# Attention block on one core: the third batch's statistics on ACT, eight split value units, and stores and row spreads moved off SP's queue

## The reference

```python
h = _group_norm(x, gn_w, gn_b)                 # 8 groups, (4, 128, 1024)
q = jnp.einsum('oc,bcn->bon', qw, h) + qb[None, :, None]
k = jnp.einsum('oc,bcn->bon', kw, h) + kb[None, :, None]
v = jnp.einsum('oc,bcn->bon', vw, h) + vb[None, :, None]
attn = jnp.einsum('bcn,bcm->bnm', q, k) / jnp.sqrt(jnp.asarray(C, x.dtype))
attn = jax.nn.softmax(attn, axis=-1)
out = jnp.einsum('bnm,bcm->bcn', attn, v)
out = jnp.einsum('oc,bcn->bon', pw, out) + pb[None, :, None]
return x + out.reshape(B, C, H, W)
```

## Time and profile before

| | us |
|---|---|
| median of 3 runs | 138.47 |
| lowest and highest | 137.95, 139.0 |
| the profiled execution | 138.43 |
| span of its profile (first to last instruction) | 136.2 |
| granted TensorE clock, mean | 1.000 |

### The profile page before, as it was taken

One profiled execution on the slowest core, in us unless ns is written; L12 is line 12 of the kernel. 1 busy time (PEld: TensorE's weight loads), 2 busy tenths in 40 slices (PEclk: granted clock), 3 DMA queues, 4 the chain that ended last, 5 costly groups with the idle time before them and its releaser, 6 DMA issues.

```text
span 136.2 us, 2258 instructions
## 1 busy us (share of the span) xinstructions
PE 127.9 (94%) x759; PEld 111.6 (82%) x759; DVE 101.1 (74%) x172; ACT 70.0 (51%) x118; POOL 40.4 (30%) x39
## 2 busy tenths in 40 slices
PE   5899999949999999999999999999999999999990
PEld 5897878827768888999898898898988999988870
DVE  0577889999998878979689989856977898140222
ACT  4054687755765673547346977474585335331000
POOL 5053005085020251305026695024049220012000
PEclk9999999999999999999999999999999999999999
DMA  4970000001998599889961898899915998989512
GB/s 139 277 278 0 0 5 0 18 23 35 197 212 178 152 216 206 188 218 216 203 188 36 196 212 189 233 204 211 199 70 118 197 212 217 239 184 212 172 39 77
DMA packets 9566, 21.00 MB, mean 154 GB/s; under 512 B 2362, under 2 KB 4052, under 8 KB 9556
## 3 DMA queue, kind: packets, MB, share of 16 engines
q1 hardware_dynamic: 8816, 20.59, 62.1%
q10 hardware_dynamic: 740, 0.28, 0.8%
HBM read 4.07 MB, written 2.11 MB: 45 GB/s over the span
## 4 chain that ended last, share of the span: by engine, by line
PE 65%; SPq 12%; DVE 9%; issue 6%; DMA 5%; DVEq 0%
PE ACC L417 24%; SPq L205 11%; PE S L336 8%; PE S L337 7%; PE S L340 7%; PE A L316 5%; DVE blocks L735 3%; PE S L375 3%; DMA pT<-blocks 2%; DMA x_sb<-x 2%; DVE s_sb L726 2%; PE S L280 2%; PE A L292 1%; DVE bn L651 1%; PE A L293 1%
## 5 line engine op out<-in xcount | busy, mean ns | idle before, releaser
L726 DVE TENSOR_SCALAR_CACHE_REDUCE s_sb<-S,row_term 128x1024 f32<-128x1024 f32 x32 | 40.9, 1279 | 12.1 <-PE S L340 11.9
L417 PE MATMUL ACC<-pT,v 128*128 128x128 f32 (+1 forms) x288 | 45.8, 310 | 0.2 <-DMA pT<-blocks 0.2
L546 ACT ACTIVATE s_sb<-s_sb,rowmin 128x1024 f32<-128x1024 f32 x32 | 36.8, 1151 | 15.5 <-DVE s_sb L726 14.5
L417 PEld LDWEIGHTS ACC<-pT,v 128*128 128x128 f32 x288 | 40.3, 191 | 3.4 <-issue 0.6
L735 DVE STREAM_TRANSPOSE blocks<-s_sb 128x1024 f32<-128x1024 f32 x28 | 34.7, 1239 | 0.0
L336 PE MATMUL S<-h_hi,g_hi 128*128 128x512 f32 x64 | 28.7, 449 | 0.3 <-issue 0.3
L337 PE MATMUL S<-h_lo,g_hi 128*128 128x512 f32 x64 | 25.1, 393 | 0.0
L340 PE MATMUL S<-h_hi,g_lo 128*128 128x512 f32 x64 | 19.9, 392 | 0.0
L887 POOL TENSOR_TENSOR xb<-rden_bc,xb 128x512 f32<-128x512 f32 (+1 forms) x7 | 8.4, 1197 | 24.6 <-DVE rden_bc L755 18.9
L340 PEld LDWEIGHTS S<-h_hi,g_lo 128*128 128x128 f32 x64 | 12.0, 188 | 2.8
L336 PEld LDWEIGHTS S<-h_hi,g_hi 128*128 128x128 f32 x64 | 12.1, 189 | 2.3 <-issue 0.4
(11 more groups left out here) (100 smaller groups left out, 145.7 us busy)
## 6 DMA issues: line engine op xcount, KB each, us to landing
pT<-blocks SPq DMA_DIRECT2D x112, 128.0 KB, 2.5
rden_bc<-row_store SPq DMA_DIRECT2D x6, 256.0 KB, 3.5
x_sb<-x SPq DMA_DIRECT2D x1, 1024.0 KB, 6.6
out<-xb SPq DMA_DIRECT2D x8, 128.0 KB, 2.7
out<-xb SPq DMA_DIRECT2D x4, 256.0 KB, 3.1
x_sb<-x SPq DMA_DIRECT2D x2, 256.0 KB, 3.0
x_sb<-x SPq DMA_DIRECT2D x1, 512.0 KB, 3.9
w_in<-weights ACTq DMA_DIRECT2D x2, 128.0 KB, 3.5
```

The source lines that it names most:

```text
L417: last = pe.matmul(to, v[:, b % 3, t, :], probs[:, :, t, :], start=(t == 0), stop=(t == KT - 1))
L546: act.activation(s_sb[:, c % 3, :], s_sb[:, c % 3, :], ACT.Exp, bias=rowmin[:, c % CH:c % CH + 1], scale=-1.0, accum_out=den[:, n % 2, k:k ...
L726: dve.tensor_scalar(s_sb[:, c % 3, :], S[:, c % 2, :], row_term[:, b % 2, i:i + 1], None, ALU.add, ALU.min, accum_out=rowmin[:, i:i + 1]). ...
```

## The change

The statistics of batch 2 go from DVE to ACT: two passes over x with an accumulated sum (`channel_means` in step 6, `channel_squares` in step 7, scratch in `pT`, for which set 2's move now waits), and the deviations move to step 8. Batch 1's scale, shift, h_hi and h come a step earlier. Split units become eight, over sets 1, 3 and 5. The last set is done by chunk (eight tiles by 128 columns each), one before and one behind units 2 and 3 of set 7, each with its own finish and store. SP keeps the moves and the last stores; `spread_rows` goes to ACT, a step behind `copy_rows`, and the stores of sets 0 to 6 to POOL, behind each residual. DVE computes its row terms directly behind the drain instead of behind its transposition.

The diff, cut to its core:

```diff
-TURN_STEPS = (3, 9, 11, 15, 19, 23, 27)
+TURN_STEPS = (3, 10, 11, 15, 19, 23, 27)
-DEVIATION_STEPS = (1, 7, 16)
-VARIANCE_STEPS = (2, 8, 17)
-EARLY_STATS_STEPS = (5, 6)
-SPLIT_SETS = (3, 5)
+DEVIATION_STEPS = (0, 8, 16)
+VARIANCE_STEPS = (1, 9, 17)
+CHANNEL_STEPS = (6, 7)
+SPLIT_UNITS = ((1, 2), (1, 3), (3, 0), (3, 2), (3, 3), (5, 0), (5, 2), (5, 3))
+SPLIT_SETS = (1, 3, 5)
+ROUND_V_STEPS = (9, 15, 23)
...
+    FIRST_QUARTERS = {FIRST[n] + 7: SPLIT_UNITS.index((n, 0)) for n in (3, 5)}
+    SECOND_QUARTERS = {FIRST[n] + 6 + u: SPLIT_UNITS.index((n, u)) for n in (3, 5) for u in (2, 3)}
...
+        chunk_sums = [S[:, 1, BANK * d:BANK * d + P] for d in range(2)]
...
         # SP
             def move_set(n):
                 sp.wait_ge(blocks_ready, FIRST[n + 1] - SETS[0])
+                if n == 2:
+                    sp.wait_ge(chan_ready, 3)
...
-            spread_rows(0)
-            move_set(1)
-            spread_rows(1)
-            for n in range(2, LS):
+            for n in range(1, LS):
                 move_set(n)
-                if n < SPREAD_BY_DMA:
-                    spread_rows(n)
-                store_set(n - 2)
-            store_set(LS - 2)
-            store_set(LS)
-            store_set(LS - 1)
+            store_chunk(0)
+            store_last_moved()
+            store_chunk(1)
...
         # PE
+            def last_chunk_unit(d):
+                for f in range(HALVES):
+                    pe.wait_ge(pair_ready[f], SETS[0] + SETS[LS])
+                pe.wait_ge(v_ready, VP * B)
+                pe.wait_ge(rowmin_ready, STEPS)
+                for t in range(KT):
+                    last = pe.matmul(chunk_sums[d], v[:, L % 3, t, :], pair_T[:, t, d, :], start=(t == 0), stop=(t == KT - 1))
                 last.then_inc(part_done, 1)
...
             value_unit(FIRST[LS - 1] + 1)
             value_unit(DIRECT)
-            value_unit(DIRECT + 1)
             value_unit(FIRST[LS - 1] + 2)
             value_unit(FIRST[LS - 1] + 3)
+            value_unit(DIRECT + 1)
...
         # ACT
+            def channel_means():
...
+                act.activation(pT[:, 0, 0:N], x_sb[:, 2, :], ACT.Identity, accum_out=chan_sums[:, 0:1]).then_inc(sums_ready, 1)
+                act.wait_ge(sums_ready, 1)
+                act.mul(chan_sums[:, 1:2], chan_sums[:, 0:1], -1.0 / N).then_inc(sums_ready, 1)
+                act.mul(chan[:, 0:1], chan_sums[:, 0:1], 1.0 / N).then_inc(sums_ready, 1)
+            def channel_squares():
+                act.wait_ge(sums_ready, 3)
+                act.activation(pT[:, 0, 0:N], x_sb[:, 2, :], ACT.Square, bias=chan_sums[:, 1:2], accum_out=chan_sums[:, 2:3])\
+                   .then_inc(sums_ready, 1)
+                act.wait_ge(sums_ready, 4)
+                act.mul(chan[:, 1:2], chan_sums[:, 2:3], 1.0 / N).then_inc(chan_ready, 1)
...
+            def round_probs(r):
+                n, u = SPLIT_UNITS[r]
+                for a in (2 * (u // 2), 2 * (u // 2) + 1):
+                    act.wait_ge(moved[n % 2][a], MOVED * ((n + 1) // 2))
+                if r > 1:
+                    act.wait_ge(part_done, unit_end(r - 2))
+                    act.wait_ge(p_lo_ready, r - 1)
+                probs, hi, lo = split_views(r)
+                act.copy(hi, probs).then_inc(p_hi_ready, 1)
...
+                if c in FIRST_QUARTERS:
+                    round_probs(FIRST_QUARTERS[c])
...
-                if late == 3 and b < L:
+                if i == 3 and b < L:
                     normalize_hi(b + 1, 0, HALVES)
-                if late == 4 and b < L:
+                if i == 4 and b < L:
                     normalize(b + 1)
+                if c - 1 in ROW_STEPS:
+                    spread_rows(ROW_STEPS.index(c - 1))
...
                 exponentials(c)
+                if c == CHANNEL_STEPS[0]:
+                    channel_means()
+                if c == CHANNEL_STEPS[1]:
+                    channel_squares()
+                if c in ROUND_V_STEPS:
+                    round_v(ROUND_V_STEPS.index(c))
+                if c == FIRST[1] + LAG:
+                    round_probs(0)
+                    round_probs(1)
...
         # DVE
+            def finish_last_chunk(d):
+                dve.wait_ge(part_done, (STEPS - 3, STEPS)[d])
...
-                if i == 3 and 0 < b < L:
+                if i == 3 and b < L:
                     shift(b + 1)
-                if c in EARLY_STATS_STEPS:
-                    half_stats(2, EARLY_STATS_STEPS.index(c))
                 if divided_in(c) is not None:
                     divide(divided_in(c))
                 drain_scores(c)
-                if c == VARIANCE_STEPS[0] + 1:
-                    shift(1)
+                if late == 0:
+                    row_terms(b, 1)
+                if late == 2:
+                    row_terms(b, 2)
+                if i == 7 and b < L:
+                    row_terms(b + 1, 0)
...
         # POOL, add_residual(n)
+                pool.wait_ge(out_ready, n + 1)
+                at = P * FIRST[n]
+                while at < P * (FIRST[n] + SETS[n]):
+                    b, first = at // N, at % N
+                    width = min(N, first + P * (FIRST[n] + SETS[n]) - at) - first
+                    pool.dma_start(out[b, :, first:first + width], xb[:, b, first:first + width]).then_inc(moved_stored, 16)
+                    at += width
...
+                if c - 1 in ROUND_V_STEPS:
+                    split_v(ROUND_V_STEPS.index(c - 1))
+                if c in FIRST_QUARTERS:
+                    split_probs(FIRST_QUARTERS[c])
+                if c in SECOND_QUARTERS:
+                    split_probs(SECOND_QUARTERS[c])
+                if c == FIRST[1] + LAG:
+                    split_probs(0)
+                    split_probs(1)
```

More of the change, by code:

```diff
@@ L152, in build @@
         A1 = psum("A1", [P, BANK])
-        sums = [ACC[:, n % 2, 0:P * SETS[n]] for n in range(LS)] + [S[:, 1, 0:PN]]
+        sums = [ACC[:, n % 2, 0:P * SETS[n]] for n in range(LS)]
+        chunk_sums = [S[:, 1, BANK * d:BANK * d + P] for d in range(2)]
         last_sums = [ACC[:, (LS - 1) % 2, 0:UW], ACC[:, LS % 2, 0:UW]]
@@ L190, in moved_view, with split_views, unit_end @@
             return pT[:, n % 2, 0:SETS[n] * N].rearrange("p (a t n) -> p a t n", a=NQ, t=KT)
+        def split_views(r):
+            n, u = SPLIT_UNITS[r]
+            part, half = u // 2, u % 2
+            probs = moved_view(n)[:, 2 * part:2 * (part + 1), PT * half:PT * (half + 1), :].rearrange("p a t n -> p t a n")
+            return (probs, *(p[:, r % 2].rearrange("p t (a n) -> p t a n", a=2) for p in (p_hi, p_lo)))
+        def unit_end(r):
+            n, u = SPLIT_UNITS[r]
+            return FIRST[n] + u + 1
         def blocks_view(n):
@@ L207, in move_set, with store_last_moved, store_chunk @@
                           .then_inc(moved[n % 2][a], 16)
[L209 to L216, removed]
-                if n < SPREAD_BY_DMA:
[L218 to L226, removed]
+            def store_last_moved():
+                sp.wait_ge(tail_out_ready, 3)
+                cs = slice(P * (DIRECT % CH - GC), P * (DIRECT % CH))
+                sp.dma_start(out[L, :, cs], xb[:, L, cs]).then_inc(stored, 16)
+            def store_chunk(d):
+                sp.wait_ge(tail_out_ready, (2, 4)[d])
+                cs = slice(P * (CH - 2 + d), P * (CH - 1 + d))
+                sp.dma_start(out[L, :, cs], xb[:, L, cs]).then_inc(stored, 16)
             for f in range(HALVES):
@@ L367, in first_set_part @@
                     last.then_inc(part_done, 1)
[L369 to L376, removed]
-                last.then_inc(part_done, 1)
@@ L387, in split_unit @@
                     t = PT * half + w
-                    pe.matmul(to, v_hi[:, t, :], p_hi[:, half, w, :], start=(t == 0), stop=False)
-                    pe.matmul(to, v_hi[:, t, :], p_lo[:, half, w, :], start=False, stop=False)
-                    last = pe.matmul(to, v_lo[:, t, :], p_hi[:, half, w, :], start=False, stop=(t == KT - 1))
+                    pe.matmul(to, v_hi[:, t, :], p_hi[:, r % 2, w, :], start=(t == 0), stop=False)
+                    pe.matmul(to, v_hi[:, t, :], p_lo[:, r % 2, w, :], start=False, stop=False)
@@ L391, in split_unit @@
+                    last = pe.matmul(to, v_lo[:, t, :], p_hi[:, r % 2, w, :], start=False, stop=(t == KT - 1))
                 last.then_inc(part_done, 1)
             def moved_unit(n, u):
-                if n in SPLIT_SETS and u > 1:
-                    split_unit(n, u - 2)
+                if (n, u) in SPLIT_UNITS:
+                    split_unit(n, u)
                     return
```

106 lines of the change are left out of this document (48 added, 58 removed).

## The result

The changed kernel takes 136.92 us, median of 20 executions (136.0 to 140.27), against 138.82 us for the kernel before, run beside it (median of 20, 137.94 to 144.54). The ratio is 0.9878, 95% interval 0.9845 to 0.991: 1.2% faster. Forecast were 136.8 us and a gain of 1.67 us; measured are 1.9 us between the medians and 1.7 us by the ratio. The profiled execution took 136.12 us with a span of 134.4 us; before it was 138.43 and 136.2. (The medians are over all executions, while the ratios leave out the slow ones, some 2 us longer: two of the changed kernel's, of 140.2 us, and elsewhere mostly such as have a mean granted clock of 0.975 to 0.988 instead of 1.00; only in experiments 3 and 6, where five of six have such a clock, these stayed in.)

A forecast was written before the change was run, and what follows sets the result against it. PE, busy 94% of the 136.2 us span, was taken as the bound. Gains 1.28 + 0.8 + 0.24 + 0.55 = 2.87 us, less 1.2 given back: 138.43 - 1.67 = 136.8 us, range 134.8 to 138.8.

The forecast's parts named there:

- The forecast's case: Whole kernel: 2.87 us gained and 1.2 us given back, 136.8 us (135.9 to 137.5), chance 0.43.
- four more split units: PE's steps: 2.80 us apart with a split unit instead of 3.12, so 4 x 0.32 = 1.28 us gained.
- early stall: PE's 1.95 us wait for the second batch's h_lo goes, but later waits leave 0.8 us gained, bounds 0 and 1.95.
- move of set 7: With SP free, the move starts when its blocks are there and PE's wait goes: 0.24 us gained.
- tail: End of kernel: smaller last DVE operations and last store, 0.65 - 0.1 = 0.55 us gained, between 0.2 and 0.9.
- given back on POOL's queue: Steps 19 and 27: two stores of 0.85 us each ahead of p_lo overrun the slack; 1.2 us lost in all.
- the sentence that PE is full from there: From scores 9, expected at 35.85 us, PE would have no gaps, so 0.8 us of the 1.95 us is kept.
- The rival of quick stores: POOL issues a store in 0.6 us or less, so neither step 19 nor 27 overruns: 135.6 us, chance 0.20.
- Moves and stores: Moves go by their issue; stores on other queues only lengthen the landing, with room except perhaps at set 6's first half.
- The spreads on ACT: Row read-backs on ACT, one step after the row's store, land beside an exponential of 1.24 us: no cost.

The follow-up runs named there:

- experiment 3: Changed kernel with the third batch's statistics back on DVE and deviations in step 7, early shift kept: 139.05 us, ratio 1.0006 to the kernel before.
- experiment 6: Kernel before with only the queues changed (POOL stores the sets, ACT reads the rows back): 140.28 us, ratio 1.0121.
- Experiment 1: Changed kernel with the four split units of before instead of eight: 137.65 us, ratio 0.9922 to the kernel before.
- experiment 4: Changed kernel with ACT's two statistics passes in steps 5 and 6 instead of 6 and 7: 136.74 us, ratio 0.9866 to the kernel before.
- experiment 5: Kernel before with only the early shift of batch 1, statistics staying on DVE: 140.04 us, ratio 0.9978.
- experiment 11: Kernel before with only the third batch's statistics moved from DVE to ACT, the late shift staying: 139.35 us, ratio 1.0039.
- experiment 2: Changed kernel with POOL's stores issued two steps later on its queue: 136.42 us, ratio 0.982 to the kernel before.
- experiment 8: Changed kernel with POOL's stores two steps later, ACT's passes in steps 5 and 6, and set 7's last move quarter issued by ACT: 138.3 us, ratio 0.997.
- experiment 9: Changed kernel with POOL's stores two steps later, those of sets 5 and 6 only after set 7's move: 135.67 us, ratio 0.9778 to the kernel before.
- experiment 7: Changed kernel with batch 2's statistics on DVE, deviations in step 8, and seven unread matmuls in step 7: 138.31 us, ratio 0.9977 to the kernel before.
- experiment 12: Kernel before with only the last set done by chunks of 128 columns: 138.16 us, ratio 0.9952.

## Why the prediction was right

The forecast's case was the one that came: each wait that it named is there, on the engine that it named. Each term of its sum can be read from the table, by distances in two profiled executions:

| term | forecast | in the profile |
|---|---|---|
| four more split units | 1.28 | 0.59 + 0.33 + 0.35 = 1.27 |
| early stall | 0.8 | 0.53 |
| move of set 7 | 0.24 | 1.18 - 0.79 = 0.39 |
| tail | 0.55 | 1.8 - 1.18 = 0.62 |
| given back on POOL's queue | -1.2 | -0.52 - 0.49 = -1.01 |
| outside the span | not seen | 0.5 |
| sum | 1.67 | 1.80 + 0.5 |

**Split units.** The difference of 3.12 and 2.80 us held; the three parts in the table are set 1 with two units, and units (3,0) and (5,0). Experiment 1 showed what the sum did not hold: PE's time saved in one step makes other waits nearer, so that the four units are worth 0.7 us by the medians and not 1.27.

**Early stall.** Value tiles at 31.74 (forecast 31.6), squares done at 35.66 (35.55 to 35.6), scores 9 at 35.96 (35.85). Scores 9 come 0.64 us earlier where the sum kept 0.8. And what failed is the sentence that PE is full from there: experiment 4 gives it 1 us more at scores 9, and by scores 11 that is gone, since PE waits for DVE in steps 9 and 10. I also named the parts of this term wrongly: I wrote that DVE is relieved and that the stall goes because of it and the earlier shift, as if each had a share. Experiments 5 and 11 show that each alone gives nothing. Of the 0.8 us 0.53 are left at scores 12.

**POOL's queue.** The right steps, and the right slack: 78.76 - 75.19 (end of the residual) - 2.42 = 1.15 us, forecast 1.17. The price of the stores was wrong. I took 0.85 us for each and 0.1 us for POOL's wait on its own residual; measured are 0.56 and 0.30. From the residual's end to the start of p_lo that makes 76.64 - 75.19 = 1.45 us, an overrun of 0.30, and the missed hand-over costs 0.2 us beyond it, which I had not counted. So the 1.2 us given back were near (1.01) by luck, with three terms off that offset each other. The rival of quick stores had the price right (0.6 us or less) and its time, 135.6 us, wrong, because 2 x 0.56 = 1.12 us lies just inside the slack only as long as the wait of 0.30 us is left out. The Trainium skill's start of about 1 us for a DMA of POOL (DMA: Bandwidth & Descriptors, Specifications, where it is a latency to the first byte) can't be read as the time that an issue holds POOL, which is 0.54 to 0.60 us in this trace and 0.77 us for the first store; no row here shows the first byte.

**Moves and stores.** This reading was wrong. From a share of 0.98 at 217 and at 268 GB/s I concluded that stores don't hold up moves. Issue does not suffer (set 7's move takes SP 10.77 us, before 10.67), but landing does, once other DMAs lie among it: 3.9 to 4.7 us beside one row spread in experiment 6, 3.0 and 3.3 us beside stores in experiment 2, and 6.23 us beside ACT's share of the move in experiment 8. The spreads on ACT, which I had put at nothing, are the first of these; in the changed kernel too set 5's DMAs issued beside one (from 91.12 on) land after 3.2 to 3.9 us, the ones ahead of them mostly after 2.4 to 2.8. In the changed kernel nobody waited for it, so the sum was not touched. With PE 0.8 us earlier (experiment 2) it cost 0.6 us, and taking the stores of sets 5 and 6 out of the move (experiment 9) gave it back. The Trainium skill has the rule which I had set aside (Trainium Kernel Development and Optimization, Key Constraints): all queues run on the same 16 DMA engines, so that a further queue saves only time of issue. Experiments 8 and 9 agree with it.

**What made the number so near.** The mechanism was right, but that 136.8 us met 136.92 so closely is luck: two things that I did not see offset each other. Outside the span there are 0.5 us less. And the profiled execution is among the fastest of its kernel: the others reach 138.0 us at a clock of 1.00, two even 140.2, and the median lies 0.8 us above it. The six of experiment 9, without stores in the last move, lie within 0.6 us. That fits transfers that land late in some executions; only one execution of each has a profile, so it is not shown.

## To carry to other kernels

A stall that is ended by a chain over several engines is priced by what is late next on each of them, not by its length: two edits that each give nothing alone may give something together, and one edit alone may only move the wait. A queue that looks free is not a free place for a DMA; count what stands behind the issue on that engine, and what else is on its way to landing, and put stores behind the last transfer that someone waits for. Where an engine is taken off the path, look again at the waits that were just covered, since they are now the gain's limit.

## What I had not expected of the hardware

- After PE had stood for 1.93 us (experiment 11), 2.09 us (experiment 3) and 2.46 us (experiment 8), its granted clock fell to the 1.2 GHz level for 3 to 4 us. In the profiles after waits of 1.95 us (before), 1.9 us (experiment 6) and 2.21 us (experiment 5) it did not fall, but other executions of these kernels have mean clocks of 0.975 to 0.988; the length of the wait alone does not tell. None of the changed kernel's is below 0.999, and its longest wait behind the start is 1.02 us. In experiment 7, with seven small matmuls in the stall (and the deviations a step later), all twelve kept it. So an edit that only moves such a wait can cost the clock, and one that shortens it can save it, which the profile of one execution at 1.00 does not show.
- All kernels with the stores on POOL's queue have 1.68 to 1.79 us around the span, in every execution, and those without (before, experiments 5, 11 and 12) 2.15 to 2.28 us. Experiment 6, which changes the queues alone, has 1.68 to 1.76. Why is open.
- SP's issue of one DMA in a move is 0.59 us by the median, and each profile has one to four of 1.3 to 2.1 us.
